# Two attention layers of a graph network run as one stream of 32 groups on one core

## The reference

```
# third layer: 12 heads of 32, encoding_bias = adj
q, k, v = x @ Wq.T, x @ Wk.T, x @ Wv.T + bv        # reshaped to heads
a = softmax(q @ k.T * 384**-0.5 + adj)             # rows that are all 0 are masked
x = layernorm(x + (a @ v) @ Wo.T + bo)
# fourth layer: 12 heads of 32, with a mask
q, k, v = x @ Wq + bq, x @ Wk + bk, x @ Wv + bv
s = q @ k.T / sqrt(32) + beta * adj;  s = where(adj > 0, s, -9e15)
x = layernorm(x + softmax(s) @ v)
```

## Time and profile before

| | |
|---|---|
| median of 3 runs | 3087.94 us (3087.86 to 3088.18) |
| the profiled execution | 3087.28 us |
| its span | 3085.2 us |
| PE busy | 2926.5 us, 95% of the span |
| DVE busy | 2301.9 us, 75% |
| POOL busy | 1375.3 us, 45% |
| ACT busy | 1155.7 us, 37% |
| DMA, mean of the 16 engines | 47 GB/s |

### The profile page before, as it was taken

One profiled execution on the slowest core, in us unless ns is written; L12 is line 12 of the kernel. 1 busy time (PEld: TensorE's weight loads), 2 busy tenths in 40 slices (PEclk: granted clock), 3 DMA queues, 4 the chain that ended last, 5 costly groups with the idle time before them and its releaser, 6 DMA issues. The chain is left out here.

```text
span 3085.2 us, 57599 instructions
## 1 busy us (share of the span) xinstructions
PE 2926.5 (95%) x22080; PEld 2491.0 (81%) x22080; DVE 2301.9 (75%) x5311; ACT 1155.7 (37%) x2369; POOL 1375.3 (45%) x1207
## 2 busy tenths in 40 slices
PE   8999999999599999999999599999999789999997
PEld 7988888889488888888887488888888677888886
DVE  6788888888557766766775688888888667777777
ACT  3344443444322222222222234434443234444443
POOL 6755576556465555555554232222222212332233
PEclk9999999999799999999999799999999999999998
DMA  5121121111211101100110111101111011111111
GB/s 141 31 68 47 50 62 58 61 47 54 87 54 49 39 25 35 49 29 25 45 49 11 55 51 45 45 23 45 45 33 36 34 37 45 46 45 46 56 45 44
DMA packets 134641, 145.98 MB, mean 47 GB/s; under 512 B 56800, under 2 KB 132320, under 8 KB 134368
## 3 DMA queue, kind: packets, MB, share of 16 engines
q1 hardware_dynamic: 134368, 142.31, 14.9%
HBM read 91.96 MB, written 50.33 MB: 46 GB/s over the span
## 5 line engine op out<-in xcount | busy, mean ns | idle before, releaser
L1908 POOL TENSOR_TENSOR l_prob<-l_prob,l_mx 128x512 f32<-128x512 f32 x192 | 200.7, 1045 | 774.9 <-DVE l_mx L1745 774.9
L1135 DVE TENSOR_TENSOR l_val<-l_ring,l_vec 64x384 f32<-64x384 f32 x512 | 284.6, 556 | 75.6 <-PE l_ring L950 68.7
L950 PE MATMUL l_ring<-whi,l_hhi 128*128 128x384 f32 x1152 | 272.8, 345 | 5.8 <-POOL wlo L79 5.8
L950 PE MATMUL l_ring<-wlo,l_hhi 128*128 128x384 f32 x1152 | 263.4, 336 | 0.0
L950 PE MATMUL l_ring<-whi,l_hlo 128*128 128x384 f32 x1152 | 263.3, 336 | 0.0
L1499 PE MATMUL l_ring<-l_hhi,whi 128*128 128x512 f32 x576 | 234.9, 408 | 9.5 <-DVE l_hlo L1725 9.2
L680 POOL TENSOR_TENSOR l_hlo<-l_hf,l_hhi 128x512 fp32r<-128x512 f32 x96 | 128.5, 1362 | 256.0 <-DVE l_hhi L477 256.0
L1499 PE MATMUL l_ring<-l_hlo,whi 128*128 128x512 f32 x576 | 228.8, 397 | 0.0
L1499 PE MATMUL l_ring<-l_hhi,wlo 128*128 128x512 f32 x576 | 228.8, 397 | 0.0
L445 ACT ACTIVATE l_mt<-l_ring 128x512 f32<-128x512 f32 x192 | 115.2, 600 | 292.0 <-PE l_ring L345 292.0
L950 PEld LDWEIGHTS l_ring<-whi,l_hhi 128*128 128x128 f32 x1152 | 200.7, 189 | 24.6 <-issue 18.6
(11 more groups left out here) (211 smaller groups left out, 7050.2 us busy)
## 6 DMA issues: line engine op xcount, KB each, us to landing
l_hf<-xt SPq DMA_DIRECT2D x16, 864.0 KB, 5.5
l_x<-x SPq DMA_DIRECT2D x16, 768.0 KB, 4.5
x<-l_za SPq DMA_DIRECT2D x16, 768.0 KB, 4.5
x<-l_zb SPq DMA_DIRECT2D x16, 768.0 KB, 3.6
l_xa<-x SPq DMA_DIRECT2D x16, 768.0 KB, 4.9
l_xb<-x SPq DMA_DIRECT2D x16, 768.0 KB, 6.5
x<-l_zfa SPq DMA_DIRECT2D x8, 768.0 KB, 3.5
x<-l_zfb SPq DMA_DIRECT2D x8, 768.0 KB, 4.3
```

Source lines behind the costliest of these rows:

```text
L950: mm = nc.tensor.matmul(ring[k % RING][:, 0:D], hh[:, c, first:first + P], ww[:, c, :], start=(j == 0), stop=(j == len(terms) - 1))
L1135: ins = nc.vector.tensor_tensor(val[half, (g + b) % GRAPHS, 0:D], ring[k % RING][half, 0:D], bias[half, :], ALU.add)
L1908: nc.gpsimd.tensor_tensor(row, row, mx[:, c, ts, :].rearrange("p t h -> p (t h)").unsqueeze(2) .broadcast_to([P, 2 * HP, S]), ALU.subtract)\
```

## The change

`heads_pass` is called once and runs 32 slots, 16 groups of the third layer and then 16 of the fourth. Function by function:

- There are two `prob` buffers, which alternate. Of group n+1 the query and key products come as pairs (query chunk, key chunk), and `chunk_scores(n+1, 0)` and `chunk_scores(n+1, 1)` stand between the outputs of group n.
- `vside`, `swap` and `sides` are gone, on PE and ACT. `values_out` writes all four quarters of a tile straight into `val`, two of them from one half of the partitions to the other.
- All four parts of a key chunk are copied by ACT; `keys_out` on DVE is gone.
- `output` has the head pairs in the outer loop and the two halves in the inner one.
- `final_apply` is on ACT; DVE only forms the shift (`final_shift`).
- The input is loaded in halves, the residual of the third layer is added in four instructions, the mask is built in place, and the banks in which the inputs are turned are others.

```diff
         q = sb("q", [P, KC, R])
         keys = sb("keys", [P, KC, GRAPHS, HP, S])
-        vside = sb("vside", [P, 2, PAIRS, HD])
         val = sb("val", [P, GRAPHS, PAIRS, 2, HO])
-        prob = sb("prob", [P, KC, T, HP, S])
+        probs = [sb(f"prob{a}", [P, KC, T, HP, S]) for a in "ab"]
         probt = [sb(f"probt{k}", [P, PAIRS, P]) for k in range(2)]
...
+            for n in range(slots):
+                if n:
+                    if n + 1 < slots:
+                        sync.wait_ge(t_done, KC * n)
+                        for half in range(2):
+                            sync.wait_ge(x_used, 2 * (n - 1) + half + 1)
+                            load_x(n + 1, half)
+                        sync.wait_ge(s_evac, UNITS * n)
+                        load_adj(n + 1)
+                    store(n - 1)
...
+            def query_key(n, k):
+                w, m = weight(n, k % 2), k // 2
+                if k >= 2:
+                    pe.wait_ge(qk_evac, 2 * KC * n + k - 1)
+                elif project(n - 2):
+                    pe.wait_ge(w_evac, T * (n - 2) + 3 + k)
+                else:
+                    pe.wait_ge(v_evac, max(T * (n - 1) + 3 + k, 0))
...
-            def sides(n, ts):
-
-                for t in ts:
-                    if project and t == 0:
-                        pe.wait_ge(olo_done, T * n)
-                    pe.wait_ge(v_evac, T * n + t + 1)
-                    if t >= 2:
-                        pe.wait_ge(side_evac, T * n + t - 1)
-                    nc.tensor.matmul(pt[t % 2][:, 0:PAIRS * HD], sh.swap[:, :],
-                                     vside[:, t % 2, :, :].rearrange("p m f -> p (m f)"),
-                                     start=True, stop=True).then_inc(side_done, 1)
+            def value(n, t):
...
-            def outputs(n, t):
+            def output(n, t):
                 pe.wait_ge(pt_evac, 2 * (T * n + t + 1))
-                pe.wait_ge(n_done, T * n + max(t - 1, 0))
-                for b in range(2):
-                    rows = slice(S * b, S * b + S)
-                    for m in range(PAIRS):
+                pe.wait_ge(v_evac, T * n + t + 1)
+                pe.wait_ge(n_done, max(T * n + t - 1, 0))
+                if t == 0 and n + 1 < slots:
+                    pe.wait_ge(lo_done, KC * (n + 2))
+                if t == 1 and project(n - 1):
+                    pe.wait_ge(olo_done, T * n)
+                for m in range(PAIRS):
+                    for b in range(2):
+                        rows = slice(S * b, S * b + S)
                         mm = nc.tensor.matmul(ot[t % 2][rows, 2 * m * HO:2 * (m + 1) * HO], probt[t % 2][:, m, rows],
                                               val[:, 2 * t + b, m, :, :].rearrange("p h f -> p (h f)"),
                                               start=True, stop=True)
                 mm.then_inc(o_done, 1)
 
...
+            for n in range(slots):
+                before, more = project(n - 1), n + 1 < slots
+                value(n, 0)
+                if before:
+                    outputs_turned(n - 1, range(0, 2))
+                value(n, 1)
+                if before:
+                    outputs_turned(n - 1, range(2, 4))
+                value(n, 2)
+                value(n, 3)
+                if more:
+                    rows_turned(n + 1, range(KC))
                 chunk_scores(n, 2)
+                if before:
+                    if n == 1:
+                        pe.wait_ge(sh.w_ready, 16)
+                    for t in range(T):
+                        result(n - 1, t)
+                if n + 1 == groups:
+                    pe.wait_ge(sh.w_ready, 19)
+                if more:
+                    query_key(n + 1, 0)
+                    query_key(n + 1, 1)
+                probs_turned(n, 0)
+                if more:
+                    query_key(n + 1, 2)
+                    chunk_scores(n + 1, 0)
+                probs_turned(n, 1)
+                output(n, 0)
+                if more:
+                    query_key(n + 1, 3)
+                probs_turned(n, 2)
+                output(n, 1)
+                if more:
+                    query_key(n + 1, 4)
+                probs_turned(n, 3)
+                output(n, 2)
+                if more:
+                    chunk_scores(n + 1, 1)
+                    query_key(n + 1, 5)
+                output(n, 3)
 
         @block.scalar
         def _(act):
...
+            def query_key(n, k):
+                c = k // 2
+                act.wait_ge(qk_done, 2 * KC * n + k + 1)
+                act.wait_ge(s_done, max(KC * (n - 1) + c + 1, 0))
+                if k % 2 == 0:
+                    parts = [(slice(0, P), q[:, c, :], ring[0][:, :])]
+                else:
+                    parts = [(part, keys[part, c, :, h, :], ring[1][part, :].rearrange("p (g j) -> p g j", j=S))
+                             for h in range(HP) for part in [slice(HD * h, HD * h + HD)]]
+                for part, out, src in parts:
+                    if project(n):
...
+            def final_apply(n):
+                act.wait_ge(fb_done, n + 1)
+                for t in range(T):
+                    ins = nc.scalar.activation(z[n % 2][:, t, :], z[n % 2][:, t, :], ACT.Identity, scale=FR[:, t:t + 1],
+                                               bias=FB[:, t:t + 1])
+                ins.then_inc(y_done, 1)
...
+            for n in range(slots):
+                before, more = project(n - 1), n + 1 < slots
+                if n + 1 == groups:
+                    act.wait_ge(col_in, 16 * 3)
+                if before:
+                    outputs_high(n - 1, range(T))
+                if more:
+                    high_parts(n + 1)
+                exponential(n, 4)
+                exponential(n, 5)
+                if more:
+                    query_key(n + 1, 0)
+                    query_key(n + 1, 1)
+                probs_out(n, 0)
+                if more:
+                    query_key(n + 1, 2)
+                if n:
+                    final_apply(n - 1)
+                probs_out(n, 1)
+                if more:
+                    query_key(n + 1, 3)
+                probs_out(n, 2)
+                if more:
+                    exponential(n + 1, 0)
+                    exponential(n + 1, 1)
+                    query_key(n + 1, 4)
+                probs_out(n, 3)
+                if more:
+                    query_key(n + 1, 5)
+                    exponential(n + 1, 2)
+                    exponential(n + 1, 3)
+            final_apply(slots - 1)
 
         @block.vector
...
+            def values_out(n, t):
+                bias = rowvec[:, 2 * (n // groups), :].rearrange("p (m q f) -> p m q f", q=2, f=HD)
+                bank = ring[t % 2]
+                dve.wait_ge(v_done, T * n + t + 1)
+                dve.wait_ge(o_done, max(T * (n - 1) + t + 1, 0))
+                src = bank[:, 0:D].rearrange("p (m q f) -> p m q f", q=2, f=HD)
+                for b in range(2):
+                    rows = slice(S * b, S * b + S)
+                    for p in range(2):
+                        ins = nc.vector.tensor_tensor(val[S * p:S * p + S, 2 * t + b, :, p, 0:HD], src[rows, :, p, :],
+                                                      bias[rows, :, p, :], ALU.add)
+                ins.then_inc(v_evac, 1)
...
+                if n:
+                    divide(n - 1, 3)
+                values_out(n, 0)
+                if before:
+                    outputs_low(n - 1, range(0, 2))
+                values_out(n, 1)
+                if before:
+                    outputs_low(n - 1, range(2, 4))
+                values_out(n, 2)
+                values_out(n, 3)
+                if more:
+                    low_parts(n + 1)
+                maxima(n, 4)
+                if before:
+                    result_out(n - 1, 0)
+                maxima(n, 5)
+                if before:
+                    for t in range(1, T):
+                        result_out(n - 1, t)
                 split_weights(sh, dve, "hi", *weights_of_slot(n))
+                if n:
+                    final_stats(n - 1)
+                if more:
+                    if n + 1 == groups:
+                        dve.wait_ge(sh.w_ready, 19)
+                    additive_mask(n + 1)
+                if n:
+                    final_shift(n - 1)
+                if more:
+                    maxima(n + 1, 0)
+                divide(n, 0)
+                if more:
+                    maxima(n + 1, 1)
+                divide(n, 1)
+                divide(n, 2)
+                if more:
+                    maxima(n + 1, 2)
+                    maxima(n + 1, 3)
+            divide(slots - 1, 3)
...
+            for n in range(slots):
+                before, more = project(n - 1), n + 1 < slots
+                if n and not before:
+                    residual(n - 1, range(T - 1, T))
+                if project(n):
+                    residual(n, range(T))
```

(19 more changed lines are left out.)

637 lines of the change are left out of this document (224 added, 413 removed).

## The result

The changed kernel takes 2987.45 us (median, 2985.25 to 2988.55), the kernel before 3088.06 in the same job: a ratio of 0.9673, 95% interval 0.9656 to 0.969. The gain is 100.6 us where the prediction had 135. The direction and the mechanism hold, and the time lies in the stated range, 2.6 us under its upper end; 34 us more come back than was reckoned.

A forecast was written before the change was run, and what follows sets the result against it. PE, 98% full in a steady group, was taken as the bound. Savings of 168.3 us, with 12.8, 18.7 and 3.5 coming back, made -133.3: span 3085.2 to 2951.9, forecast 2953 us, range 2915 to 2990 (8 in 10).

The forecast's parts named there:

- Outputs, 32.4 ns for 57: Output matmuls on PE, halves in turn: 0.59 us saved a tile, 128 tiles, -75.5 us.
- outputs no faster: Rival: output records stay at 57 ns, +75.5 us, 3029 us; chance 0.08.
- Swap and seam: Swap matmuls go, -42.2 us, with PE's waits around them, -18.6; idle stretch between third and fourth layer goes, -32.0.
- Slots with a projection, +0.8: PE waits for DVE's result copy behind the sixth maximum: 0.8 us in each of 16 slots, +12.8 us.
- Slots without one, +1.3: PE waits for ACT's key copies, 0.4 us for the last chunk and 0.9 for the first: +18.7 us.
- Start, +3.5: First slot: scores wait for DVE 2.8 us, first values' copies 2, less 1.5 of an earlier wait: +3.5 us.
- End, 0: End of the kernel, 40.1 us, same chain of maximum, exponential, outputs, residual, norm: no cost.
- Loads, at no cost: Input's half loads: second half asked for about 2.0 us into a slot, needed at 6.8; no cost.
- The seam stays: Rival: slots around group 16 wait for weights or loads as before, +32 us, 2985 us; chance 0.01.
- More new waits: Rival: norm and key copies on ACT hold turned tiles and PE, 1.5 us in 30 slots, +45, 2998 us; chance 0.15.
- No new waits: Rival: DVE and ACT keep up everywhere, so +35 us falls away, 2918 us; chance 0.12.
- The slower one: Rival: DVE's value writes across partition halves take 0.75 us instead of 0.353, 3126 us; chance 0.03.

The follow-up runs named there:

- the edits: Changed kernel with query copy earlier, fourth-layer keys split between ACT and DVE, reciprocal written in PSUM, second result and second turned-probability copy earlier: 2947.48 us.
- the fifth edit: On ACT, second copy of turned probabilities ahead of the norm of the group before; not run alone, only with four others on the changed kernel: 2947.48 us.
- all together: Changed kernel with five edits at once (query copy, keys on two engines, reciprocal, second result, second turned-probability copy): 2947.48 us, ratio to before 0.9547.
- query copy first: Changed kernel with ACT's copy of the next group's first query chunk ahead of the sixth unit's exponential: 2979.59 us.
- reciprocal in PSUM: Changed kernel with the third layer's reciprocal written in place in PSUM, so the masked multiply reads one operand there: 2976.18 us.
- the last experiment: Kernel with one part of the last keys on DVE (2941.6 us), first scores behind first outputs now only in slots without a projection: 2939.49 us.
- four small edits: On the changed kernel: query copy earlier (2979.59 us), with it fourth-layer keys on two engines (2972.27); separately reciprocal in PSUM (2976.18), second result ahead of sixth maximum (2973.87).

## Where the prediction was right and where not

**Outputs, 32.4 ns for 57.** Right in the pace (31.3), and with it the rival "outputs no faster" falls, and so does, as the prediction read it, the rule of the Trainium skill for weight loads within one row group; that section also names loads into a background weight buffer, and no run tells whether these are such. The term of 0.59 us a tile came out as 0.52: 0.07 is lost beside the outputs, see below. The whole term of 75.5 us is not collected in either order: the alternation is worth 46 us in the old one and 50 in the new one, and the rest is among the waits that came.

**Swap and seam.** No swap rows, no seam: the windows show the clock at 1.00 and PE 98.7% busy over 2400 to 2500. The swap's 60.8 us (42.2 and 18.6 for waits around it) could not have been taken as a sum in the old order: alone they gave 14, which the text did not see. What they are worth by themselves in the new order was not run. The waits that they stood for were in part replaced there by others for the same value copies (0.59 us a slot ahead of the third values, until the reciprocal was changed).

**Slots with a projection, +0.8.** This term failed. Above the 40.26 us that are left of 44.70 by the terms that go, the slot has 1.89. Of these 1.41 were taken away by the edits (40.74): one where the forecast put it, the result copy behind the sixth maximum (0.82 when it was taken away, walked at 0.3), and one that it passed over, value copies behind a masked reciprocal held up by POOL (0.78 when taken away; the two together, with the fifth edit, gave 0.2 less than their sum). The prediction had POOL's hold in its upper end, by the other instruction of the earlier trace rows, and then leaned towards the walk.

**Slots without one, +1.3.** Right in the engine and in the reason (four key parts of 0.68 us), too small: the slot is 2.03 above 32.53. That it came within 0.7 is in part luck. The two waits that it named, 0.4 for the last chunk and 0.9 for the first, cost 0.49 and 0.35 from start to start, less than its 1.3; a third that it did not name, the query copy behind the exponential, costs 0.60, and the other 0.6 are not waits with a bracket.

**What the walks left out.** Both compared when an engine is ready with the end of PE's work by the clock of the rows. A wait read as 0.62 or 0.36 us then costs 0.86 or 0.6. And 0.5 to 0.6 us a slot have no bracket: without one a slot of the third layer has 40.74, of which 0.24 is the gap behind the results, not 40.26, and one of the fourth 32.81 + 0.30 = 33.11, not 32.53 (0.27 of it beside the second values, where a wait too short for a bracket can't be excluded). The starts show where. Outputs take 0.75 us ahead of scores and 0.85 ahead of a product, whose first matmul then has 0.34 until the next instead of 0.23. Scores and outputs write half of the array's columns, products all. Moving the scores next to the outputs removed one such place and 0.30 us, as it should by these starts. But the change of columns is not shown to be the cause: behind a turned block, which uses all columns like the product that follows, this one's first matmul has 0.32 as well (1940.32 to 1940.64 in the kernel after), and so has the first query product behind the results. It may be the kind of matmul; no run separates the two.

**Start, +3.5.** The brackets after 1719 us are 0.38, 0.38, 3.19, 2.19 and 1.90 us, 8.0 together, where the forecast had 4.8; the 1.5 that it took off (1.54 before) are gone indeed. That is some 3 us more:

```profile
1747.68 3.40 PE L1489 MATMUL h_scores<-h_keys,h_q 128*64 128x256 f32 x16 [3.19 <-DVE h_proba L1703]
1756.59 0.79 PE L1472 MATMUL h_ring<-whi,h_hhi 128*128 128x384 f32 x3 [2.19 <-DVE h_val L1724]
1771.70 0.50 PE L1464 MATMUL h_ring<-h_hhi,whi 128*128 128x512 f32 x1 [1.90 <-ACT h_q L1612]
```

The first two are the ones forecast (2.8 and 2); the last, the query copy behind the first slot's exponentials, was not foreseen. With the 28.2 us of the slots this is 31 of the 31.6, or some 29 if the shorter slots are counted as they are.

**End, 0.** From the last scores to the end 28.4 us, before 28.9 (3056.35 to 3085.2): right in the sum, and in part by luck. The outputs are cheaper and the granted clock is 0.81 there against 0.72 before, but ACT has the norm's four instructions ahead of the second copy of turned probabilities, and PE waits 1.33 us for it ahead of the third turned block. With the copy first (all together, the last row) this wait is gone, and the end takes 27.3 us:

```profile
2963.76 2.50 ACT L1641 ACTIVATE h_za<-h_za,h_small 128x384 f32<-128x384 f32 x4 [1.11 <-DVE h_small L1781]
```
```profile
2966.78 0.85 PE L1506 MATMUL h_pt<-ident,h_probb 128*128 128x128 f32 x6 [1.33 <-ACT h_probt L1634]
```
```profile
2930.09 1.20 PE L1516 MATMUL h_pt<-ident,h_probb 128*128 128x128 f32 x6
```

The end also moves with the clock: with the same order of work it took 30.7 us at a granted clock of 0.66 (query copy first) and 30.5 at 0.71 (reciprocal in PSUM).

**Loads, at no cost.** Right in nearly every slot. PE waits for the load of an input once in the kernel after, 0.23 us, and once or twice in three of the later kernels, at most 1.04 us; in the last two never.

**The rivals.** By its number "The seam stays" (2985) is nearest, and it is refuted: no break is left. "More new waits" (2998) has nearly the size but not the place: the norm's instructions on ACT, 0.70 us each instead of under 0.63, hold no turned tile in a steady slot, and only one at the end. "No new waits" is what the last experiment comes near to: 2936.9 of span, 20 above this rival's 2951.9 - 35.0 = 2916.9. Of these 16 x 0.48 + 15 x 0.28 = 12 are in the slots and some 3 at the start; the rest has no place that was found. The slower one is refuted by the 355 ns.

## What to carry to other kernels

Where PE is over 95% busy, a term that shortens its work is worth its size only if the engines behind it can follow there: try the walk with the order as it stands and with the order changed, and price each wait from start to start of PE's rows, since here the bracket left out 0.07 to 0.27 us. If several short waits are left, take them one by one: here four small edits added up within some 3 us, and gave 40 us beside the change's 101. Let small VectorE instructions read one operand from PSUM where GpSimd works beside them.

## What was not expected of the hardware

- A VectorE instruction of 12 columns with both inputs in SBUF: 0.98 us beside a GpSimd instruction, 0.17 with one input in PSUM beside the same one.
- 66-column matmuls with output halves in turn run at 31.3 ns, against 57 ns with the two halves in blocks; 24 of them take 0.1 us more ahead of a product than ahead of scores, and the product's first matmul 0.1 us more than its others.
- ScalarE's 384-column Identity with a scale and a bias for each partition takes 0.70 us, longer than its exponential of 512 columns.
